# Ten small moves around a TensorE that hardly waits: gate total, identity transposes, unit 2, one eviction, one h and one rank sum

## The chip, the cores and the metric

The kernel runs on one core of a Trainium2 chip. The metric is the device time of one execution in microseconds (us), the median of several runs. Four engines do the work: TensorE (PE, matmuls; its weight loads are shown as PEld), VectorE (DVE), ScalarE (ACT) and GpSimd (POOL). SyncE (SP) issues most of the transfers (DMA) from the chip's memory. The engines run side by side and wait for each other through semaphores. TensorE's clock has two levels, 1.2 and 2.4 GHz; the profile shows the granted clock as a share of the higher one.

## The reference

`L0_attn_x` has 1024 tokens of 512 numbers. Three parts share the layernorm `xn`: a block whose weights come from 4-bit codes (NF4) with scales and low-rank additions, a feed-forward block whose weights are a mean plus one coefficient times a sign, and a product of the two.

```python
xn = layernorm(x)                                   # 1024 x 512
# block 1: dequantised weights W = NF4[codes] * scales, each with a low-rank term A, B
q, k, v = lin_lora(xn, Wq), lin_lora(xn, Wk), lin_lora(xn, Wv)
x1 = xn + lin_lora((q + k + v) / 3, Wo)
s  = x1 + lin_lora(silu(lin_lora(x1, Wg)) * lin_lora(x1, Wu), Wd)   # inner width 1792
# block 2: each of the three weights is one of these
def binary_diff_weight(w, base):
    d = w - base
    coeff = mean(abs(d))                            # one number for the whole weight
    return base + coeff * sign(d)
h = silu(xn @ W1.T) * (xn @ W3.T)                   # inner width 1792
g = silu(h @ W2.T)
out = x + s * g
```

## The kernel before, in words

The activations lie transposed, 512 features in four blocks of 128 rows (hc 0 to 3) and 1024 tokens in two halves of 512 (th 0 and 1). Every value that TensorE reads is split into a high and a low part, so that a full-precision product is three matmuls (high by high, high by low, low by high). A matmul group of one chunk of 128 inner rows and one half is 4 x 3 = 12 matmuls of 128 x 512.

The inner width of 1792 is 14 chunks for the feed-forward block (chunks 0 to 13) and 14 for the NF4 block (chunks 14 to 27, `B0` = 14). The order is written out by hand, engine by engine; there is no scheduler. Each engine has one list of instructions, and an instruction that waits holds up all behind it on its engine.

**The head.** VectorE computes the layernorm's statistics and normalises eight token tiles (`normalise(t)`), TensorE transposes them against an identity matrix (`ident`), ScalarE copies the high part out (`x_high`), VectorE subtracts to get the low part (`x_low`, counted by the semaphore `xT_lo`). Between these, TensorE runs `warm(bank, count)`: transposes of the identity whose result nobody reads. While the weights still come in, the three coefficients are summed: the first four chunks of each weight are "units" (unit 0 to 3 gate, 4 to 7 up, 8 to 11 down), the rest is scanned (`scan_subtract`, `scan_signs`, sums of absolute values on ScalarE or VectorE). GpSimd subtracts some units (`unit_subtract`), and `early_low` makes the low part of the mean of chunk 0; it waits for `scan_subtract(1)`.

The coefficient of the gate weight is not known when TensorE could begin. So chunk 0's gate is computed in two: `early_mean(th)` multiplies by the mean, 12 matmuls each, and `early_signs(th)` by the signs, 8 matmuls each, 16 in all; then `total(GATE)`, one small matmul with a matrix of ones, sums the partial sums over the rows. VectorE turns its result into the coefficient (`take_coeff`), makes unit 1 (`split_make`, `split_low`) and joins the two products of chunk 0 (`early_scale`, `early_add`), for ScalarE's `silu(0, th)`. The same with `total(UP)`, which stands in the middle of the gate matmuls of chunk 4, and `total(DOWN)`. The sums that `total` reads are ready when `take_part` has run on VectorE; it waits for all sums of that weight, the last on ScalarE is `unit_sum(7)` for the up weight.

`unit_make(u)` adds coefficient times sign (VectorE), `unit_high(u)` copies the high part (ScalarE), `unit_low(u)` makes the low part (VectorE); then `project(u, ...)` may start on TensorE.

**The middle and the end.** `STAGES` lists the order: a number is a phase (gate and up products of a chunk), "D0" to "D9" are down products of a group of two or three chunks, "X" makes x1. In a phase of the NF4 block VectorE has, beside `h_make` and `h_low` (the product of the two branches and its low part, for th 0 and 1), four "bends" (`nf4_bend`, 1536 wide, each on a ramp that ScalarE made) and one scaling (`nf4_scale`) that dequantise a later chunk, `rank_part` (`rank_add` and `lora_add`: the low-rank product that TensorE has just put into two banks is added), and `gu_low` and `dn_low`, the low parts of the next chunk's weights. `rank_gu` on TensorE may write its banks when ScalarE has evicted the down tiles that lay there (`y_evict`).

The lines that the steps below touch: the head's list on VectorE and on ScalarE (each written as plain calls), the start of TensorE's list with `WARM`, and in `phase(k)` on VectorE

```python
                if BEFORE[k] == k - 1:
                    h_make(k - 1, 1)
                    third_scale(k - 1)
                make(k)
                steps(k, 0)
                if BEFORE[k] == k - 1:
                    h_low(k - 1, 1)
                ...
                rank_part(k)
                ...
                steps(k, 1, 0, 1)
                split(k)
```

Of the kernel before, what the change touches and what calls it, by code (L numbers as in the profile page):

```python
# [10 lines left out]
TT = TOKENS // P  # L11
# [25 lines left out]
RING = 5  # L37
WARM = {-1: 12, 1: 8, 3: 5, 7: 7}
FIRST_TILES = 3
# [33 lines left out]
DOWN_RING = [(DOWN2, DOWN0, DOWN1, GATE0, GATE1) if g == 0 else (DOWN0, DOWN1, DOWN2, UP0, UP1) if g == FFN_GROUPS - 1  # L73
             else (DOWN0, DOWN2, UP0, DOWN1, UP1) for g in range(len(GROUPS))]
LATE_PHASES = [B0 + 1, B0 + 2, B0 + 3, B0 + 4]

# [69 lines left out]
def block_kernel(nc, x, xT_in, w_in, mean_in, codes_in, scales_in, codes_attn, scale_qkv_in, scale_o_in,  # L146
# [9 lines left out]
    with ctx:  # L156
# [530 lines left out]
        def _(act):  # L687
# [215 lines left out]
            def down_stage(g):  # L903
# [3 lines left out]
                steps(stage, 0)  # L907
                for t in range(TT):
                    y_evict(g, t)
                    if g == 0:  # L910
# [8 lines left out]
                    elif t >= 4 and stage == "D3":  # L919
                        steps(stage, 1, t, t + 1 if t < TT - 1 else None)  # L920
                    elif t == 1:
                        if stage in SPLIT_IN:
                            gu_high(SPLIT_IN[stage])
                    elif t == 2:
                        steps(stage, 1, 1, 2)
                    elif t == 3:
                        if stage in SPLIT_IN:
                            dn_high(SPLIT_IN[stage])
                    else:
                        steps(stage, 1, t - 2, t - 1 if t < TT - 1 else None)  # L930
# [56 lines left out]
            split_high(1)  # L987
            scan_signs(3)
            unit_signs(3)
            silu(0, 0)  # L990
            unit_high(2)
            silu(0, 1)
            scan_signs(4)
            silu(1, 0)
# [83 lines left out]
        def _(dve):  # L1078
# [298 lines left out]
            def phase(k):  # L1377
                if BEFORE[k] == k - 1:
                    h_make(k - 1, 1)
                    third_scale(k - 1)  # L1380
                make(k)
                steps(k, 0)
                if BEFORE[k] == k - 1:
                    h_low(k - 1, 1)
                if k == FIRST + 1:
                    dn_low(k)
                rank_part(k)
                if k == FIRST:
# [11 lines left out]
                if k - 1 in LATE_PHASES:  # L1400
                    late_low_rows(LATE_PHASES.index(k - 1))
                    h_low(k, 0)
                for s in ATTN_STEPS[k][1][2:3]:
                    attn_step(s)
                for s in NF4_STEPS[k][1][2:3]:
                    nf4_bend(s)
                if k - 1 not in LATE_PHASES:
# [85 lines left out]
            for t in range(4, TT):  # L1493
                normalise(t)
            scan_subtract(1)
            for t in range(4):
                x_low(t)
# [14 lines left out]
            split_low(1)  # L1512
            early_scale(0)
            early_add(0)
            early_scale(1)
            unit_make(2)
            early_add(1)
            scan_subtract(5)
            unit_low(2)
            unit_make(3)  # L1520
# [101 lines left out]
        def _(pe):  # L1622
# [3 lines left out]

            pe.wait_ge(const_ready, 3)
            warm(side_ps, WARM[-1])
            for t in range(TT):
# [5 lines left out]
                if t in (1, 3):  # L1635
                    warm(side_ps, WARM[t])
            pe.wait_ge(xT_lo, 1)
            warm(early_ps[0], WARM[TT - 1])

# [10 lines left out]
            def early_signs(th):  # L1650
                pe.wait_ge(unit_sign, 1)
                for hc in range(HC):
                    for x_part in (HI, LO):
                        last = nc.tensor.matmul(up_ps[th][:, :], sign_T[:, hc * P:(hc + 1) * P],
# [206 lines left out]
            early_signs(0)  # L1861
            total(GATE)
            early_signs(1)
# [84 lines left out]
```

## Time and profile before

| | |
|---|---|
| median of 3 runs | 536.0 us (535.98 to 536.23) |
| the profiled execution | 536.4 us, span 534.6 us |
| PE busy | 522.1 us, 98% of the span, 2337 matmuls |
| DVE busy | 442.0 us, 83% |
| ACT busy | 328.5 us, 61% |
| POOL busy | 94.8 us, 18% |
| mean granted clock of PE | 0.997 |

The span is the time from the first to the last instruction in the trace, and the execution's own time is 1.8 us longer. A busy share says little where engines take turns: what counts is when TensorE stands still, or runs at the lower clock, and who ended that wait.

### The profile page before, as it was taken

The numbers are of one execution on the slowest core, as the hardware profiler recorded it, in microseconds if no ns is written. First come the engines' busy times: TensorE is split into PE (matmuls) and PEld (weight loads), VectorE is DVE, ScalarE is ACT, GpSimd is POOL, SyncE is SP. The second block draws the span as 40 slices with busy tenths as digits, with TensorE's granted clock in tenths as the row PEclk, the third lists the DMA queues.
The fourth block names the chain that finished last, engine by engine and source line by source line (L and its number), as shares of the span: only waits on it lengthen the run. The fifth ranks groups of instructions, "written<-read, shape, count | busy, mean of one in ns | idle before, by whom it ended". The sixth has DMA issues, their size and how long they took to land.

```text
span 534.6 us, 6499 instructions
## 1 busy us (share of the span) xinstructions
PE 522.1 (98%) x2337; PEld 432.2 (81%) x2337; DVE 442.0 (83%) x520; ACT 328.5 (61%) x455; POOL 94.8 (18%) x106
## 2 busy tenths in 40 slices
PE   5899999999999999999999999999999999999997
PEld 4678888888888888888888888887888888888886
DVE  6988998988896998865898988999989898874446
ACT  2979978557546555446648557867876585464310
POOL 1311002003100310022003121300310040004590
PEclk9899999999999999999999999999999999999999
DMA  8999904045811491059238994932582377127503
GB/s 337 397 402 403 377 4 154 25 132 99 189 50 63 70 229 58 1 104 224 51 75 159 243 219 100 195 83 63 97 163 58 75 157 148 29 51 161 135 20 139
DMA packets 31744, 76.73 MB, mean 144 GB/s; under 512 B 3872, under 2 KB 7296, under 8 KB 31584
## 3 DMA queue, kind: packets, MB, share of 16 engines
q1 hardware_dynamic: 21632, 57.42, 34.4%
q0 software_dynamic: 9792, 18.88, 20.4%
q8 instruction: 19, 0.31, 0.2%
q14 instruction: 13, 0.11, 0.1%
q10 hardware_dynamic: 288, 0.02, 0.0%
HBM read 53.23 MB, written 2.10 MB: 103 GB/s over the span
## 4 chain that ended last, share of the span: by engine, by line
PE 87%; DVE 8%; issue 3%; DMA 1%; ACT 1%; SPq 0%; DVEq 0%; ACTq 0%
PE up_ps L1692 25%; PE gate_pair L1692 22%; PE down_pair L1733 10%; PE up_ps L1733 9%; PE down_ps L1733 7%; PE side_ps L1776 2%; PE down_pair L1692 2%; DVE acc L1339 2%; PE down_pair L1645 1%; PE up_ps L1853 1%; PE gate_pair L1853 1%; PE down_pair L1853 1%; DMA xn<-in_x 1%; PE down_pair L1815 1%; PE gate_pair L1733 1%
## 5 line engine op out<-in xcount | busy, mean ns | idle before, releaser
L1692 PE MATMUL up_ps<-xT,gu 128*128 128x512 f32 x648 | 152.3, 390 | 0.4 <-DVE gu L1173 0.2
L1692 PE MATMUL gate_pair<-xT,gu 128*128 128x512 f32 x624 | 148.4, 390 | 0.0
L1692 PEld LDWEIGHTS up_ps<-xT,gu 128*128 128x128 f32 x648 | 121.4, 188 | 26.4 <-DVE gu L1173 0.6
L1692 PEld LDWEIGHTS gate_pair<-xT,gu 128*128 128x128 f32 x624 | 117.0, 188 | 24.6 <-DVE gu L1164 0.5
L651 POOL DMA_DIRECT2D y<-y_part x64 | 55.3, 875 | 339.9 <-ACT y_part L815 338.7
L802 ACT ACTIVATE h<-up_ps 128x512 fp32r<-128x512 f32 x52 | 31.0, 597 | 111.1 <-DVE up_ps L1231 58.0
L861 ACT ACTIVATE ramp<-codes,bend_bias 128x1536 f32<-128x1536 uint8 x56 | 88.1, 1579 | 0.9 <-DMA codes<-in_codes 0.9
L1339 DVE SCALAR_TENSOR_TENSOR acc<-ramp,acc 128x1536 f32<-128x1536 f32 x42 | 73.7, 1754 | 4.4 <-ACT ramp L861 4.0
L1733 PE MATMUL down_pair<-h,dn 128*128 128x512 f32 x249 | 60.9, 389 | 0.0
L1733 PEld LDWEIGHTS down_pair<-h,dn 128*128 128x128 f32 x249 | 46.7, 188 | 9.8
L1236 DVE TENSOR_TENSOR h<-up_ps,h 128x512 fp32r<-128x512 f32 x52 | 35.8, 689 | 19.7 <-ACT h L802 19.4
L1733 PE MATMUL up_ps<-h,dn 128*128 128x512 f32 x210 | 51.5, 389 | 0.0
L1733 PEld LDWEIGHTS up_ps<-h,dn 128*128 128x128 f32 x210 | 39.4, 188 | 8.2
L1733 PE MATMUL down_ps<-h,dn 128*128 128x512 f32 x159 | 39.2, 390 | 0.0
L841 ACT ACTIVATE attn_ramp<-attn_codes,bend_bias 128x1024 f32<-128x1024 uint8 x32 | 36.8, 1150 | 0.0
L797 ACT ACTIVATE silu_gate<-gate_pair 128x512 f32<-128x512 f32 x48 | 28.3, 589 | 12.9 <-PE gate_pair L1692 12.7
L1733 PEld LDWEIGHTS down_ps<-h,dn 128*128 128x128 f32 x159 | 29.9, 188 | 6.1
L1292 DVE SCALAR_TENSOR_TENSOR attn_acc<-attn_ramp,attn_acc 128x1024 f32<-128x1024 f32 x24 | 29.3, 1220 | 3.0 <-ACT attn_ramp L841 2.9
L1339 DVE SCALAR_TENSOR_TENSOR acc<-ramp,codes 128x1536 f32<-128x1536 f32 x14 | 24.5, 1753 | 4.4 <-ACT ramp L861 4.4
L1231 DVE SCALAR_TENSOR_TENSOR up_ps<-up_ps,silu_gate 128x512 f32<-128x512 f32 x28 | 19.4, 693 | 9.2 <-PE up_ps L1692 9.2
L1349 DVE SCALAR_TENSOR_TENSOR acc<-acc,scale 128x1536 f32<-128x1536 f32 x14 | 24.6, 1756 | 0.4
L815 ACT ACTIVATE y_part<-up_ps 128x512 f32<-128x512 f32 x23 | 13.9, 603 | 12.5 <-PE up_ps L1733 12.5
(227 smaller groups left out, 648.1 us busy)
## 6 DMA issues: line engine op xcount, KB each, us to landing
y<-y_part POOLq DMA_DIRECT2D x64, 256.0 KB, 5.0
scale<-in_scales SPq DMA_DIRECT2D x28, 384.0 KB, 5.5
scan_w<-in_w SPq DMA_DIRECT2D x15, 512.0 KB, 10.9
base<-in_mean SPq DMA_DIRECT2D x9, 768.0 KB, 4.8
scan_mean<-in_mean SPq DMA_DIRECT2D x9, 512.0 KB, 9.7
silu_gate<-in_mean SPq DMA_DIRECT2D x6, 512.0 KB, 12.2
codes<-in_codes SPq DMA_DIRECT2D x14, 192.0 KB, 5.6
xn<-in_x SPq DMA_DIRECT2D x4, 512.0 KB, 4.9
```

What stands on the lines that cost most here:

```text
L651: pool.dma_start((y if g < FFN_GROUPS else y2)[:, hq, sl], y_slot(q), accum_op=ALU.add).then_inc(y_added[q % Y_SLOTS], 16)
L797: nc.scalar.activation(silu_buf(k, th), ps[:, :], ACT.Silu, scale=1.0 if k < B0 else UNIT_STEP).then_inc(silu_done, 1)
L802: nc.scalar.activation(h_part(k, HI, th), up_bank(k, th)[:, :], ACT.Copy).then_inc(h_hi, 1)
L841: nc.scalar.activation(attn_ramp[:, s % 2, :, :], attn_codes[:, a % 2, :, :], ACT.Prelu, bias=bend_bias[:, j:j + 1], scale=slope, alpha=le ...
L861: nc.scalar.activation(ramp[:, s % 2, :], codes[:, k % 2, :], ACT.Prelu, bias=bend_bias[:, j:j + 1], scale=slope, alpha=left).then_inc(nf4 ...
L1231: nc.vector.scalar_tensor_tensor(up_ps[th][:, :], up_ps[th][:, :], UNIT_STEP, silu_buf(k, th), ALU.mult, ALU.mult).then_inc(h_made, 1)
L1236: nc.vector.tensor_tensor(h_part(k, LO, th), up_bank(k, th)[:, :], h_part(k, HI, th).bitcast(f32), ALU.subtract).then_inc(h_lo, 1)
L1292: nc.vector.scalar_tensor_tensor(attn_acc[:, a % 2, :, :], attn_ramp[:, s % 2, :, :], end, attn_codes[:, a % 2, :, :] if j == 0 else attn_ ...
L1339: nc.vector.scalar_tensor_tensor(acc[k % 3][:, :], ramp[:, s % 2, :], end, codes[:, k % 2, :] if j == 0 else acc[k % 3][:, :], ALU.min if ...
L1349: nc.vector.scalar_tensor_tensor(acc[k % 3][:, :], acc[k % 3][:, :], UNIT_START, scale[:, :], ALU.add, ALU.mult).then_inc(nf4_scaled, 1)
L1692: last = nc.tensor.matmul(ps[:, :], w[:, w_part, hc * P:(hc + 1) * P], xT[:, x_part, hc, th * HALF:(th + 1) * HALF], start=(hc == 0 and w_ ...
L1733: last = nc.tensor.matmul(down_bank(g, t)[:, :], dn[:, k % DN_SLOTS, w_part, hq * P:(hq + 1) * P], h_part(k, h_p, th), start=(k == ks[0] a ...
```

## The change

In the head: the identity transposes go from 12 ahead of the first tile, 8 after the second, 5 after the fourth and 7 after the eighth to 8, 8, 7 and 18. The first 8 wait for the first half of the statistics (`ln_step`), and the last 18 come as 12, 3 and 3 after the first, second and third `x_low`. `x_low(0)` comes ahead of `scan_subtract(1)` on VectorE. `total(GATE)` moves from behind the first sign product into the second one, behind its fourth matmul. `unit_make(2)` and `unit_low(2)` come ahead of both `early_add`, and `scan_subtract(5)` comes between these two; on ScalarE `unit_high(2)` comes ahead of `silu(0, 0)`, and `scan_signs(4)` ahead of `silu(0, 1)`.

Later: in "D4" the eviction of tile 6 comes ahead of the ramp of the stage's fourth NF4 step. For phase 18, `rank_part` comes one phase earlier (in phase 17, ahead of the bend that stood there, which moves into phase 18), and `h_make(18, 1)` and `h_low(18, 1)` come ahead of a bend and of a scaling.

```diff
-WARM = {-1: 12, 1: 8, 3: 5, 7: 7}
+WARM = {-1: 8, 1: 8, 3: 7}
+WARM_LOW = {1: 12, 2: 3, 3: 3}
...
+H_AHEAD = [18]
+RANK_AHEAD = [18]
...
                 for t in range(TT):
+                    if stage == "D4" and t == 6:
+                        y_evict(g, t)
+                        steps(stage, 1, 3, 4)
+                        continue
                     y_evict(g, t)
...
-                    else:
+                    elif stage != "D4" or t != 5:
                         steps(stage, 1, t - 2, t - 1 if t < TT - 1 else None)
...
             scan_signs(3)
+            unit_high(2)
             unit_signs(3)
             silu(0, 0)
-            unit_high(2)
+            scan_signs(4)
             silu(0, 1)
-            scan_signs(4)
             silu(1, 0)
...
             def phase(k):
-                if BEFORE[k] == k - 1:
+                if k - 1 in H_AHEAD:
+                    h_low(k - 1, 1)
+                    third_scale(k - 1)
+                elif BEFORE[k] == k - 1:
                     h_make(k - 1, 1)
-                    third_scale(k - 1)
+                    if k not in RANK_AHEAD:
+                        third_scale(k - 1)
                 make(k)
                 steps(k, 0)
-                if BEFORE[k] == k - 1:
+                if BEFORE[k] == k - 1 and k - 1 not in H_AHEAD:
                     h_low(k - 1, 1)
...
-                rank_part(k)
+                if k in RANK_AHEAD:
+                    for s in NF4_STEPS[k - 1][1][2:3]:
+                        nf4_bend(s)
+                        nf4_scale(s)
+                else:
+                    rank_part(k)
...
+                if k in H_AHEAD:
+                    h_make(k, 1)
                 for s in ATTN_STEPS[k][1][2:3]:
                     attn_step(s)
-                for s in NF4_STEPS[k][1][2:3]:
-                    nf4_bend(s)
+                if k + 1 in RANK_AHEAD:
+                    rank_part(k + 1)
+                else:
+                    for s in NF4_STEPS[k][1][2:3]:
+                        nf4_bend(s)
...
                 normalise(t)
+            x_low(0)
             scan_subtract(1)
-            for t in range(4):
+            for t in range(1, 4):
                 x_low(t)
...
             early_scale(0)
+            unit_make(2)
+            early_scale(1)
+            unit_low(2)
             early_add(0)
-            early_scale(1)
-            unit_make(2)
+            scan_subtract(5)
             early_add(1)
-            scan_subtract(5)
-            unit_low(2)
             unit_make(3)
...
             pe.wait_ge(const_ready, 3)
+            pe.wait_ge(ln_step, 1)
             warm(side_ps, WARM[-1])
...
-            pe.wait_ge(xT_lo, 1)
-            warm(early_ps[0], WARM[TT - 1])
+            for low, count in WARM_LOW.items():
+                pe.wait_ge(xT_lo, low)
+                warm(early_ps[0], count)
...
             def early_signs(th):
                 pe.wait_ge(unit_sign, 1)
                 for hc in range(HC):
+                    if th == 1 and hc == 2:
+                        total(GATE)
...
             early_signs(0)
-            total(GATE)
             early_signs(1)
```

TensorE's list at the end of the head, before: the last identity transposes (`L1625`), the mean product (`L1645`, both halves), the sign products (`L1654`) with the total (`L1661`) between them, and the gate of chunk 1 (`L1692`).

```order
L1625 MATMUL down_pair<-ident 128x128 x7
L1645 MATMUL down_pair<-xT,gu 128x512 x24
L1654 MATMUL up_ps<-xT,dn 128x512 x8
L1661 MATMUL side_ps<-abs_part,ones 128x1
L1654 MATMUL up_ps<-xT,dn 128x512 x8
L1692 MATMUL gate_pair<-xT,gu 128x512 x24
```

The same place in the changed kernel; the names are the same, the line numbers have moved on.

```order
L1647 MATMUL down_pair<-ident 128x128 x18
L1669 MATMUL down_pair<-xT,gu 128x512 x24
L1680 MATMUL up_ps<-xT,dn 128x512 x12
L1687 MATMUL side_ps<-abs_part,ones 128x1
L1680 MATMUL up_ps<-xT,dn 128x512 x4
L1718 MATMUL gate_pair<-xT,gu 128x512 x24
```

The total now has twelve sign matmuls ahead of it and four behind it, where it had eight and eight.

VectorE's list behind the coefficient, before: `early_scale` (`TENSOR_SCALAR`), `early_add` (`down_pair`), `unit_make(2)` (the first `unit_st`), `scan_subtract(5)`, `unit_low(2)` (`gu`), `unit_make(3)`.

```order
L1476 TENSOR_SCALAR silu_gate<-up_ps,coeff 128x512
L1481 TENSOR_TENSOR down_pair<-down_pair,silu_gate 128x512
L1476 TENSOR_SCALAR silu_gate<-up_ps,coeff 128x512
L1148 SCALAR_TENSOR_TENSOR unit_st<-unit_st,coeff 128x512
L1481 TENSOR_TENSOR down_pair<-down_pair,silu_gate 128x512
L1084 TENSOR_TENSOR scan_w<-scan_w,scan_mean 128x1024
L1173 TENSOR_TENSOR gu<-unit_st,gu 128x512
L1148 SCALAR_TENSOR_TENSOR unit_st<-unit_st,coeff 128x512
```

The same instructions in the changed kernel.

```order
L1497 TENSOR_SCALAR silu_gate<-up_ps,coeff 128x512
L1155 SCALAR_TENSOR_TENSOR unit_st<-unit_st,coeff 128x512
L1497 TENSOR_SCALAR silu_gate<-up_ps,coeff 128x512
L1180 TENSOR_TENSOR gu<-unit_st,gu 128x512
L1502 TENSOR_TENSOR down_pair<-down_pair,silu_gate 128x512
L1091 TENSOR_TENSOR scan_w<-scan_w,scan_mean 128x1024
L1502 TENSOR_TENSOR down_pair<-down_pair,silu_gate 128x512
L1155 SCALAR_TENSOR_TENSOR unit_st<-unit_st,coeff 128x512
```

The low part of unit 2 has moved from seventh to fourth, and the second `early_add` from fifth to seventh, behind the scan.

VectorE's list at the passage from phase 17 to phase 18, before: `h_low(17, 0)`, the first bend of a chunk (`acc<-ramp,codes`), `h_make(17, 1)`, `h_low(17, 1)`, `rank_add`, `lora_add`, the next bend, `gu_low(19)`.

```order
L1236 TENSOR_TENSOR h<-up_ps,h 128x512
L1339 SCALAR_TENSOR_TENSOR acc<-ramp,codes 128x1536
L1231 SCALAR_TENSOR_TENSOR up_ps<-up_ps,silu_gate 128x512
L1236 TENSOR_TENSOR h<-up_ps,h 128x512
L1215 TENSOR_TENSOR acc<-acc,down_pair 128x4x2x128
L1221 TENSOR_TENSOR acc<-acc,side_ps 128x512
L1339 SCALAR_TENSOR_TENSOR acc<-ramp,acc 128x1536
L1202 TENSOR_TENSOR gu<-acc,gu 128x2x512
```

The same place in the changed kernel.

```order
L1243 TENSOR_TENSOR h<-up_ps,h 128x512
L1222 TENSOR_TENSOR acc<-acc,down_pair 128x4x2x128
L1228 TENSOR_TENSOR acc<-acc,side_ps 128x512
L1238 SCALAR_TENSOR_TENSOR up_ps<-up_ps,silu_gate 128x512
L1243 TENSOR_TENSOR h<-up_ps,h 128x512
L1346 SCALAR_TENSOR_TENSOR acc<-ramp,codes 128x1536
L1346 SCALAR_TENSOR_TENSOR acc<-ramp,acc 128x1536
L1209 TENSOR_TENSOR gu<-acc,gu 128x2x512
```

The rank sum has moved ahead of the second half of h, and the two bends of the same accumulator now follow each other directly.

## Rows read from the trace of the kernel before

**Rows 1.** The page, busy time of each engine.

```profile
PE 522.1 (98%) x2337; PEld 432.2 (81%) x2337; DVE 442.0 (83%) x520; ACT 328.5 (61%) x455; POOL 94.8 (18%) x106
```

**Rows 2.** PE timeline of the head: start, length, engine, line, [idle before <-releaser].

```profile
18.87 0.98 PE L1625 MATMUL down_pair<-ident 128*128 128x128 f32 x7 [1.08 <-DVE xT L1129]
20.75 7.34 PE L1645 MATMUL down_pair<-xT,gu 128*128 128x512 f32 x24 [0.90 <-DVE xT L1129]
...
29.75 0.28 PE L1661 MATMUL side_ps<-abs_part,ones 128*128 128x1 f32 x2
...
32.01 5.73 PE L1692 MATMUL gate_pair<-xT,gu 128*128 128x512 f32 x24
37.95 5.74 PE L1692 MATMUL up_ps<-xT,gu 128*128 128x512 f32 x24 [0.21 <-DVE gu L1173]
43.52 5.60 PE L1692 MATMUL down_pair<-xT,gu 128*128 128x512 f32 x24
...
51.01 0.28 PE L1661 MATMUL side_ps<-abs_part,ones 128*128 128x1 f32 x2
```

**Rows 3.** Stretches: length, busy PE, PEld, DVE, ACT, POOL, clock, DMA, GB/s.

```profile
14.30:17.80 3.50, 2.91 (x24) 2.32 (x22) 3.50 (x6) 3.48 (x6) 0.00 (x0) 1.00 1.03 411
17.80:21.00 3.20, 1.23 (x8) 1.02 (x9) 3.20 (x6) 3.20 (x7) 2.63 (x3) 1.00 1.03 412
21.10:24.40 3.30, 3.30 (x9) 2.58 (x8) 3.30 (x6) 3.02 (x8) 2.14 (x2) 0.50 1.03 402
...
37.10:49.40 12.30, 12.09 (x53) 9.69 (x52) 12.21 (x14) 12.14 (x25) 2.60 (x2) 1.00 1.03 404
```

**Rows 4.** DVE timeline of the head.

```profile
16.99 1.22 DVE L1084 TENSOR_TENSOR scan_w<-scan_w,scan_mean 128x1024 f32<-128x1024 f32 x1
...
21.72 1.49 DVE L1084 TENSOR_TENSOR scan_w<-scan_w,scan_mean 128x1024 f32<-128x1024 f32 x1
...
23.73 0.68 DVE L1129 TENSOR_TENSOR xT<-side_ps,xT 128x512 fp32r<-128x512 f32 x1
...
32.26 0.74 DVE L1476 TENSOR_SCALAR silu_gate<-up_ps,coeff 128x512 f32<-128x512 f32 x1
...
35.57 1.72 DVE L1084 TENSOR_TENSOR scan_w<-scan_w,scan_mean 128x1024 f32<-128x1024 f32 x1
...
49.46 0.16 DVE L1136 TENSOR_REDUCE abs_part<-abs_sums 128x1 f32<-128x9 f32 x1
```

**Rows 5.** POOL timeline of the head.

```profile
19.61 2.52 POOL L637 TENSOR_TENSOR unit_st<-unit_st 128x512 f32<-128x512 f32 x2
...
34.42 1.79 POOL L637 TENSOR_TENSOR unit_st<-unit_st 128x512 f32<-128x512 f32 x1 [9.84 <-DMA unit_st<-in_mean]
```

**Rows 6.** ACT timeline of the head, `silu(1, 0)`.

```profile
37.13 0.59 ACT L797 ACTIVATE silu_gate<-gate_pair 128x512 f32<-128x512 f32 x1
```

**Rows 7.** Timeline of all engines at the end of stage D4.

```profile
293.14 1.60 ACT L861 ACTIVATE ramp<-codes,bend_bias 128x1536 f32<-128x1536 uint8 x1
...
294.62 0.60 ACT L815 ACTIVATE y_part<-down_pair 128x512 f32<-128x512 f32 x1
...
295.27 0.53 PEld L1815 LDWEIGHTS down_pair<-B_gu,A_gu 96*128 96x128 f32 x4 [0.47 <-ACT y_part L815]
```

**Rows 8.** DVE timeline of phases 17 and 18 and stage D6.

```profile
352.97 1.75 DVE L1339 SCALAR_TENSOR_TENSOR acc<-ramp,codes 128x1536 f32<-128x1536 f32 x1
...
359.99 1.22 DVE L1202 TENSOR_TENSOR gu<-acc,gu 128x1024 fp32r<-128x1024 f32 x1
...
387.75 3.62 DVE L1339 SCALAR_TENSOR_TENSOR acc<-ramp,acc 128x1536 f32<-128x1536 f32 x2
```

**Rows 9.** PE timeline of phase 19.

```profile
361.61 5.60 PE L1692 MATMUL gate_pair<-xT,gu 128*128 128x512 f32 x24
367.05 2.88 PE L1692 MATMUL up_ps<-xT,gu 128*128 128x512 f32 x12
370.12 3.01 PE L1692 MATMUL up_ps<-xT,gu 128*128 128x512 f32 x12 [0.19 <-DVE h L1236]
```

## The prediction

> **What bounds the kernel now.** I read the page first: PE is busy for 98% of the span [rows 1], so only its waits and its stretches at the lower clock can be won, and whatever holds it up elsewhere costs the full amount. The table of waits names few ends of PE's idle time, so I went to its timeline in the head [rows 2] and to the two later places that the change touches [rows 7 to 9].
>
> The reader is to see four things in [rows 2] and [rows 3]. First, the mean product takes 7.34 us for 24 matmuls where a later group of 24 takes 5.60: from 21.1 to 24.4 the granted clock is 0.50. The stretch ahead of it had PE busy for 1.23 of 3.20 us. Second, the gate total runs at 29.75 and the gate of chunk 1 starts at 32.01, 2.26 us later: total, coefficient, make, high and low part follow each other on VectorE and ScalarE with nothing to shorten them. Third, the gate of chunk 2 waits at 37.95 for the low part of unit 2. Fourth, the up total at 51.01 comes 1.4 us after its sums were ready (49.46 plus 0.16 [rows 4]).
>
> A group's normal spacing is 5.44 us (361.61 to 367.05 [rows 9]), 0.227 a matmul. After a stall a group is longer: 37.95 to 43.52 is 5.57, so a restart costs 0.13 on top of the wait.
>
> **The head, up to the gate total.** Adding identity transposes costs little: 7 took 0.98, 0.14 each with the last one's tail. The 18 fit into the gaps in which PE waits for `x_low`: PE has done its last tile at about 17.8, and the mean product starts at 20.75 only because the fourth `x_low` ends just ahead. `x_low(0)` is moved ahead of `scan_subtract(1)`, but the sum of work up to the fourth `x_low` is the same, so 20.75 stays. If the cover were gone (clock low while they run), they would take twice as long and delay the mean by up to 1 us.
>
> With them PE is busy for some 2.3 of those 3.2 us. The stretch 14.3 to 17.8, with 2.91 of 3.50 busy and transposes alone, was followed by full clock; 1.23 of 3.20 was followed by half. I take it that the clock stays up, as 2.3 of 3.2 (0.72) lies nearer to 0.83 than to 0.38.
>
> The Trainium skill (TensorE: Matmul & The Clock Gate, Part 4: PE-mode transpose) says that work in transpose mode does not count as busy in the same way and does not bring the full clock. The trace speaks against it, since the 24 PE instructions of 14.3 to 17.8 are all transposes and the clock was 1.00. By the page the time would be that of the last rival below.
>
> What does the full clock give? The first half of the mean product ends at 20.75 + 0.1 + 12 x 0.227 = 23.6. The second half reads the second half of the tokens, whose last `x_low` ended at 23.73 + 0.68 = 24.41 [rows 4]; at the lower clock PE came later than that, so nobody saw this wait. Now it is the next wait: PE starts at 24.5. From there to the total the old order has 20 matmuls (12 mean, 8 sign), the new one 24: 24 x 0.227 + 0.1 = 5.55, so the total runs at 30.05, 0.3 **later** than before, though the clock is doubled. In the old place it would run at 29.1. The four matmuls cost 0.9, since everything behind the total hangs on it.
>
> There is a second delay. GpSimd's `early_low` waits for `scan_subtract(1)`, which now comes one `x_low` later, 0.60 us. GpSimd then runs three subtractions without a gap, two of them in the row of 2.52 us from 19.61 [rows 5], the last one until 22.13. `scan_subtract(2)` at 21.72 took 1.49 instead of 1.22 (16.99 [rows 4]): it lay for 0.41 us under GpSimd's. The one at 35.57 lay under GpSimd's for 0.64 (34.42 + 1.79 = 36.21) and took 1.72, 0.50 more. So the extra is the overlap less 0.14. With GpSimd 0.60 later the overlap is 1.01, the extra 0.87, against 0.27 before: the last `x_low` ends 0.60 later still, and the total runs at 30.65, **0.9 later**. If the overlap does not grow, it is 0.3; those are the bounds. I take 0.9, since two rows show the same relation. And if the clock does fall at 21.1 as before, the second half of the mean isn't late, and the four matmuls alone cost 0.9: the same value by another way.
>
> **Unit 2 and the up total.** Moving `unit_low(2)` ahead takes it from 37.2 to about 5 us behind the total, 2 us ahead of its need. The stall at 37.95 is gone: 32.01 to 37.95 is 5.94, a restarted group is 5.57, so 0.37 plus the restart of 0.13, **0.5 won** there.
>
> But `early_add(1)` and with it `silu(0, 1)` are late. Counted from the total's start: `early_scale(0)` at 2.5 (32.26), `unit_make(2)` 0.7 later, then ScalarE's `unit_high(2)` between make and low (0.74 + 0.63 and two hand-overs), so `unit_low(2)` at 4.6; half a microsecond under GpSimd's subtraction, which `scan_subtract(5)` paid before; `early_add(0)` at 5.7, `scan_subtract(5)` at 6.3, `early_add(1)` at 7.4 to 8.1; then `silu(0, 1)` and at 8.6 `silu(1, 0)`. Before, `silu(1, 0)` was at 37.13 [rows 6], 7.4 behind the total. ScalarE is 1.2 us late from there, and between 37.1 and 49.4 it is busy for 12.14 of 12.30 us, VectorE for 12.21 [rows 3]: nothing takes that up, and VectorE waits for ScalarE's `unit_high(3)`, so it is as late. The up sums are ready at 49.62 + 1.2 = 50.85 (counted on the old total), and PE, 0.5 ahead, is there at 50.5 and waits until 50.9. Of the 0.5 only **0.1** is left; the bounds are 0 and 0.5. The waiting total holds up PE's whole queue.
>
> The head's sum is 0.9 - 0.1 = +0.8.
>
> **D4 and phases 17 to 19.** The eviction of tile 6 at 294.62 holds up the rank matmuls (0.47 at the weight loads, some 0.3 in PE's spacing). It moves ahead of the ramp at 293.14 [rows 7]: 0.3 won. The ramp is 0.48 later (an eviction's turn), and VectorE's bend waits for each ramp, so VectorE is 0.48 later from 295 on; up to phase 18 it and ScalarE wait only for each other, so it stays late.
>
> In phase 17 the rank sum changes places with a bend. From 352.97 to the low part of chunk 19 at 359.99 [rows 8] VectorE has the same instructions in either order, but the two bends of one accumulator now follow directly: two such take 3.62, 1.87 from start to start instead of 1.67, so 0.2 more. `gu_low(19)` ends at 359.99 + 1.22 + 0.48 + 0.2 = 361.9. PE needs it at 361.61 [rows 9], or at 361.3 with the 0.3 won: a new stall of 0.6 and 0.13. In return `h_low(18, 1)` is a bend and a scaling earlier, and the stall at 370.12 goes (367.05 + 12 x 0.227 = 369.77, so 0.35 and 0.13). Sum: -0.3 + 0.7 - 0.5 = **-0.1**, bounds -0.8 (VectorE not late) and +0.4. Behind it VectorE is 0.7 late, with waits of 2 us to take it up.
>
> **The sum.** 0.8 - 0.1 = +0.7 on the profiled execution's 536.4 (span 534.6 and 1.8 around it): 537.1. The median of the runs is 536.0, 0.4 below that execution, so I forecast **536.7**. About 0.2%, 1.07 us, is what a measurement of this kernel can tell from no change; the forecast lies within it.
>
> **The rivals.**
> - The waits behind do not come (GpSimd does not delay `scan_subtract(2)`, or ScalarE catches up): for it speaks that the rows show each only once or twice. +0.3 or +0.9 - 0.5, less 0.1: 536.1 to 536.3. Chance 0.2.
> - All stalls taken out stay out: 0.3 - 0.5 - 0.8 = -1.0, 535.0. It needs VectorE at its old times at 49.5 and at 361. Chance 0.07.
> - Slower: the clock falls in the new gap ahead of the mean's second half (23.6 to 24.5 or 25.1). The one fall cost 7.34 - 5.60 = 1.7. [...] 536.7 + 1.7 = 538.4. Chance 0.12.
> - The transposes do nothing for the clock. Then 18 of them take 0.21 to 0.28 each, the mean starts up to 1 us later and at the lower clock: 536.7 + 1.0 = 537.7. This is what the page's rule would do; chance 0.05.
>
> **How the numbers follow.** The forecast with its own spread (536.3 to 537.2) has 0.5; the rest, 0.06, is for waits that I did not see. Over 537.07 lie the two slow rivals, the forecast's upper edge and some of the rest: 0.25. Under 534.93 lies half of the second rival at most and a little of the rest: 0.05. Same: 0.7. The range from 535.7 to 537.8 leaves out the clock's fall and the case of 535.0.
>
> **What would show it.** Right: granted clock 1.00 from 20.8 on; the mean product split by a wait near 24.5 to 25.1; the gate total near 30.6; no wait at 38; a wait at the up total near 51.8; a wait ahead of chunk 19's gate, none in its up product. Wrong: a gate total before 29.7, an up total that doesn't wait, or a clock of 0.50 in 24.5 to 28.

## The result, and the profile after

| | before | changed |
|---|---|---|
| median of 11 runs | 536.09 us (535.93 to 536.59) | 537.38 us (537.29 to 537.54) |
| the profiled execution | 536.4 us, span 534.6 | 537.38 us, span 535.5 |
| mean granted clock in it | 0.997 | 1.000 |

The changed kernel takes 1.0023 times as long (95% interval 1.0014 to 1.0032): slower by 1.3 us. The forecast of 536.7 us was 0.7 short. The time lies within the stated range of 535.7 to 537.8, but the rise of 1.29 is more than the 1.07 us that the prediction took as the least that can be told from no change.

The page, busy time of each engine (before: [rows 1]):

```profile
PE 519.4 (97%) x2346; PEld 430.2 (80%) x2346; DVE 443.5 (83%) x520; ACT 328.8 (61%) x455; POOL 94.4 (18%) x106
```

PE is busy for 2.7 us less, and the span is 0.9 us longer: the work went faster (the mean product alone takes 5.97 instead of 7.34), and the waits grew by more.

The stretches of the head (before: [rows 3]). The columns are the length, the busy time of PE, PEld, DVE, ACT and POOL, the granted clock, the DMA share and GB/s.

```profile
17.80:21.00 3.20, 2.80 (x20) 2.12 (x20) 3.20 (x5) 3.20 (x7) 2.01 (x2) 1.00 1.03 414
21.10:24.40 3.30, 2.64 (x12) 1.86 (x10) 3.30 (x5) 2.40 (x6) 2.14 (x3) 1.00 1.04 403
37.10:49.40 12.30, 12.30 (x56) 10.20 (x55) 11.06 (x12) 11.97 (x21) 2.59 (x2) 1.00 1.03 403
```

The granted clock stays at 1.00. In the third stretch PE no longer waits, and now VectorE does (11.06 busy where it was 12.21).

PE's timeline of the head, changed kernel (start, length, engine, line, operation, and in brackets the idle time before it and who ended it; before: [rows 2]):

```profile
17.75 1.53 PE L1647 MATMUL down_pair<-ident 128*128 128x128 f32 x12
19.49 1.14 PE L1647 MATMUL down_pair<-ident 128*128 128x128 f32 x6 [0.20 <-DVE xT L1136]
20.77 2.97 PE L1669 MATMUL down_pair<-xT,gu 128*128 128x512 f32 x12
25.19 3.00 PE L1669 MATMUL down_pair<-xT,gu 128*128 128x512 f32 x12 [1.44 <-DVE xT L1136]
28.03 2.88 PE L1680 MATMUL up_ps<-xT,dn 128*128 128x512 f32 x12
30.75 0.28 PE L1687 MATMUL side_ps<-abs_part,ones 128*128 128x1 f32 x2
30.89 1.18 PE L1680 MATMUL up_ps<-xT,dn 128*128 128x512 f32 x4
33.03 5.76 PE L1718 MATMUL gate_pair<-xT,gu 128*128 128x512 f32 x24 [0.96 <-DVE gu L1171]
38.62 5.60 PE L1718 MATMUL up_ps<-xT,gu 128*128 128x512 f32 x24
44.06 5.60 PE L1718 MATMUL down_pair<-xT,gu 128*128 128x512 f32 x24
49.50 2.20 PE L1718 MATMUL gate_pair<-xT,gu 128*128 128x512 f32 x9
51.81 0.38 PE L1687 MATMUL side_ps<-abs_part,ones 128*128 128x1 f32 x2
52.05 3.65 PE L1718 MATMUL gate_pair<-xT,gu 128*128 128x512 f32 x15
```

The mean product runs at full speed and then waits 1.44 us for the last `x_low`. The gate total comes at 30.75 instead of 29.75, the gate of chunk 1 at 33.03 instead of 32.01. The wait at chunk 2 is gone (38.62, with no bracket), and the up total at 51.81 is only 0.80 later than before. It does wait: nine matmuls from 49.50, at 0.227 each, are through at 51.54, and its sums are ready at 51.75 (51.59 and 0.16 in the next rows), so PE stands for 0.27.

VectorE's rows that answer to [rows 4], and `unit_low(3)`, which now waits:

```profile
21.74 2.11 DVE L1091 TENSOR_TENSOR scan_w<-scan_w,scan_mean 128x1024 f32<-128x1024 f32 x1
...
24.37 0.68 DVE L1136 TENSOR_TENSOR xT<-side_ps,xT 128x512 fp32r<-128x512 f32 x1
...
35.39 1.00 DVE L1180 TENSOR_TENSOR gu<-unit_st,gu 128x512 fp32r<-128x512 f32 x1
...
42.39 0.69 DVE L1180 TENSOR_TENSOR gu<-unit_st,gu 128x512 fp32r<-128x512 f32 x1 [1.21 <-ACT gu L753]
...
51.59 0.16 DVE L1143 TENSOR_REDUCE abs_part<-abs_sums 128x1 f32<-128x9 f32 x1
```

GpSimd's subtractions (before: [rows 5]) and ScalarE's `silu(1, 0)` (before: [rows 6]):

```profile
20.22 2.55 POOL L640 TENSOR_TENSOR unit_st<-unit_st 128x512 f32<-128x512 f32 x2
...
34.52 1.33 POOL L640 TENSOR_TENSOR unit_st<-unit_st 128x512 f32<-128x512 f32 x1 [9.31 <-DMA unit_st<-in_mean]
```

```profile
39.26 0.59 ACT L800 ACTIVATE silu_gate<-gate_pair 128x512 f32<-128x512 f32 x1
```

`scan_subtract(2)` lies under GpSimd's two subtractions until 22.77 and takes 2.11 us. ScalarE comes to `silu(1, 0)` 2.1 us later than before, 1.1 of it beyond the delay of the total.

VectorE and PE at the passage from phase 17 to phase 19 (before: [rows 8, 9]):

```profile
358.05 1.75 DVE L1346 SCALAR_TENSOR_TENSOR acc<-ramp,codes 128x1536 f32<-128x1536 f32 x1
359.91 1.76 DVE L1346 SCALAR_TENSOR_TENSOR acc<-ramp,acc 128x1536 f32<-128x1536 f32 x1
361.59 1.22 DVE L1209 TENSOR_TENSOR gu<-acc,gu 128x1024 fp32r<-128x1024 f32 x1
```

```profile
356.75 5.60 PE L1718 MATMUL up_ps<-xT,gu 128*128 128x512 f32 x24
...
362.86 5.76 PE L1718 MATMUL gate_pair<-xT,gu 128*128 128x512 f32 x24 [0.51 <-DVE gu L1209]
368.45 5.60 PE L1718 MATMUL up_ps<-xT,gu 128*128 128x512 f32 x24
```

There is a new wait ahead of chunk 19's gate, and the 24 matmuls of its up product run through, where before they were split at 370.12.

### The profile page after: what moved, and what is told of

It reads as the page before. It is cut to its first block, busy times and chain, and to the rows that moved or that the text cites. A ratio compares the mean times of both kernels' runs of the same rounds, so it can differ in the third digit from the quotient of the medians.

```text
span 535.5 us, 6518 instructions
## 1 busy us (share of the span) xinstructions
PE 519.4 (97%) x2346; PEld 430.2 (80%) x2346; DVE 443.5 (83%) x520; ACT 328.8 (61%) x455; POOL 94.4 (18%) x106
## 4 chain that ended last, share of the span: by engine, by line
PE 89%; DVE 7%; issue 2%; ACT 1%; DMA 1%; SPq 0%; DVEq 0%
PE up_ps L1718 25%; PE gate_pair L1718 25%; PE down_pair L1759 11%; PE up_ps L1759 9%; PE down_ps L1759 7%; PE side_ps L1802 2%; DVE scan_w L1091 1%; PE up_ps L1879 1%; PE gate_pair L1879 1%; PE down_pair L1879 1%; PE down_pair L1718 1%; DMA xn<-in_x 1%; PE down_pair L1841 1%; PE gate_pair L1759 1%; PE down_pair L1774 1%
```

## The experiments

Each was timed beside the kernel before, whose median was 536.1 to 536.2 each time. None leaves out work that the result needs. "Changed" is the changed kernel's 537.38.

**1. The gate total back in its place**, all else as changed.

```diff
-                    if th == 1 and hc == 2:
-                        total(GATE)
...
             early_signs(0)
+            total(GATE)
             early_signs(1)
```

> The changed kernel with the gate total back behind the first sign product (eight sign matmuls ahead of it instead of twelve), all else as changed. Theory: the four sign matmuls ahead of the total cost 0.9 us and all that follows up to the up total hangs on it: gate total at 29.85 instead of 30.75, gate of chunk 1 at 32.1 instead of 33.03, up total 0.9 earlier, time 537.4 - 0.9 = 536.5. Rival: the later part of the head is set by transfers or by ScalarE's own list, so that the up total stays at 51.8: 537.4.

Measured: 536.68, 0.70 less. The gate total is at 29.99 and the gate of chunk 1 at 32.26, in a trace whose first statistics of the tokens on VectorE (their start waits for a transfer) stand at 4.52 instead of 4.33; so the total is 0.9 earlier, as expected. The up total still waits a little:

```profile
51.22 0.38 PE L1685 MATMUL side_ps<-abs_part,ones 128*128 128x1 f32 x2 [0.31 <-DVE abs_part L1143]
```

The four sign matmuls cost 0.9 at the total. 0.7 of it reaches the end; the rest stays in VectorE's list, where `scan_subtract(5)` now starts at 35.82, inside GpSimd's subtraction, and takes 1.72.

**2. The denser transposes alone**, on the kernel before, with the change's waits for `ln_step` and `xT_lo` ahead of them.

```diff
-WARM = {-1: 12, 1: 8, 3: 5, 7: 7}
+WARM = {-1: 8, 1: 8, 3: 7}
+WARM_LOW = {1: 12, 2: 3, 3: 3}
```

> The kernel before with the denser identity transposes alone (8, 8, 7 and 12 + 3 + 3); x_low(0), the total, unit 2 and the later edits stay as before. Theory: the granted clock stays at 1.00 and the gate total comes at 29.2 instead of 29.75, but GpSimd's unit subtraction at 34.4 does not move, so scan_subtract(5) lies under it for 1.2 us instead of 0.64 and takes 2.2 to 2.3 instead of 1.72; the low part of unit 2 and PE's restart at 38 come no earlier: 536.0 to 536.1, no change. Rival 1: all that follows the total moves with it: 536.1 - 0.55 = 535.5. Rival 2: without the moved x_low(0) the transposes leave a wider gap and the clock falls as before: total at 29.75, 536.1.

Measured: 536.12, ratio 0.9998 (0.9990 to 1.0007). The number is that of the theory, the reason is not. VectorE and GpSimd:

```profile
35.33 1.72 DVE L1085 TENSOR_TENSOR scan_w<-scan_w,scan_mean 128x1024 f32<-128x1024 f32 x1
```

```profile
34.42 1.55 POOL L638 TENSOR_TENSOR unit_st<-unit_st 128x512 f32<-128x512 f32 x1 [9.52 <-DMA unit_st<-in_mean]
```

The scan does not grow: GpSimd's subtraction had itself been held up by `unit_make(2)`, which now ends earlier, so it ends at 35.97 instead of 36.21. Measured from the first statistics on VectorE (4.60 here, 4.28 before) PE is some 0.6 earlier from the gate total to the end of the trace. Then why is the time the same? The runs of the kernel before answer it. Of its 33 runs beside this experiment 14 had a mean granted clock of 1.000 and a median of 536.04, 12 had 0.997 and 536.38, and 7 had 0.993 or 0.994 and 536.08. The profile that I had read is one of the 0.997 (536.4). All 11 runs with denser transposes have 1.000, and none of the 120 runs of all kernels with them is under 0.999. I read this so: the fall of the clock in the mean product does not come in every run of the kernel before, but in about a third of them, and costs them 0.3; the median holds little or nothing of it. Two things stay open: only one run with 0.997 was profiled, so where the clock fell in the others is not shown, and the two traces differ by 0.6 where the medians by clock differ by 0.3.

**3. `x_low(0)` back behind `scan_subtract(1)`**, all else as changed.

```diff
-            x_low(0)
             scan_subtract(1)
-            for t in range(1, 4):
+            for t in range(4):
```

> The changed kernel with x_low(0) back behind scan_subtract(1) on VectorE. Theory: GpSimd's subtractions start 0.6 earlier, scan_subtract(2) takes 1.49 instead of 2.11, the mean's second half starts at 24.55 instead of 25.19 and the gate total comes at 30.1 instead of 30.75; all behind follows: 537.4 - 0.65 = 536.75. Rival: the clock falls at 21.1, since the first identity transposes behind the first x_low come later: the mean's first half takes 5.1, and the total comes at 30.75 or later: 537.4.

Measured: 537.32, 0.06 less. `scan_subtract(2)` takes 1.53, the mean's second half starts at 24.50, the total at 30.06, all as expected, and by the up total nearly all of it is lost. VectorE, GpSimd and PE:

```profile
34.68 1.58 DVE L1180 TENSOR_TENSOR gu<-unit_st,gu 128x512 fp32r<-128x512 f32 x1
```

```profile
34.42 1.30 POOL L640 TENSOR_TENSOR unit_st<-unit_st 128x512 f32<-128x512 f32 x1 [9.91 <-DMA unit_st<-in_mean]
```

```profile
51.68 0.38 PE L1686 MATMUL side_ps<-abs_part,ones 128*128 128x1 f32 x2 [0.69 <-DVE abs_part L1143]
```

GpSimd's subtraction of the next unit starts when its transfer lands, at 34.4 to 34.7 in every profile, whatever the total does. `unit_low(2)`, 0.7 earlier, starts inside it, takes 1.58 instead of 1.00, and with `early_add(0)` at 36.19 instead of 36.31 VectorE is where it was. PE, ahead by 0.7, waits for the sums. The theory was right as far as the total and wrong behind it. How narrow this is shows beside experiment 1, whose gate of chunk 1 starts at nearly the same time (32.26, here 32.32). Its `unit_low(2)` starts at 34.61, 0.07 ahead of GpSimd's subtraction (34.68 in that trace), and takes 0.69; its up total is at 51.22 instead of 51.68. Three of the 11 runs of experiment 1 take 537.07 to 537.24, the others 536.46 to 536.68; whether GpSimd came first in those three is not shown.

**4. Without the D4 edit**, all else as changed.

```diff
-                    if stage == "D4" and t == 6:
-                        y_evict(g, t)
-                        steps(stage, 1, 3, 4)
-                        continue
...
-                    elif stage != "D4" or t != 5:
+                    else:
```

> The changed kernel without the edit in D4 (the eviction of tile 6 behind the fourth step's ramp, as before). Theory: PE waits 0.3 more at 296 for the rank matmuls, but VectorE is 0.48 earlier from there on, the low part of chunk 19's weights comes in time and PE's stall of 0.78 at 362.9 goes: 537.4 + 0.33 - 0.78 = 536.9 to 537.0. Rival: the ramp's delay does not reach phase 19 (the stall there is the rank sum's alone): 537.4 + 0.33 = 537.7.

Measured: 537.35, no change; neither theory nor rival. VectorE is 0.49 earlier from D4 on, but in phase 17 it waits for PE's rank product ahead of `rank_add`, and PE's stall at chunk 19 comes to its end at the same moment as in the changed kernel:

```profile
354.35 1.22 DVE L1218 TENSOR_TENSOR acc<-acc,down_pair 128x1024 f32<-128x1024 f32 x1 [0.40 <-PE down_pair L1837]
```

```profile
362.86 1.43 PE L1714 MATMUL gate_pair<-xT,gu 128*128 128x512 f32 x5 [0.20 <-DVE gu L1205]
```

**5 and 6. Of the later edits only the earlier h of phase 18 (5), and all but the earlier rank sum (6).**

```diff
-RANK_AHEAD = [18]
+RANK_AHEAD = []
```

Experiment 5 takes back the D4 edit as well, as in experiment 4.

> The changed kernel without the D4 edit and without the earlier rank sum of phase 18, so that of the later edits only the earlier h of phase 18 is left. Theory: the eviction's delay on VectorE and the rank sum's wait for PE each hold the low part of chunk 19's weights late by themselves, and only without both does PE's stall of 0.78 at 362.9 go, while 0.33 comes back at 296: 537.4 + 0.33 - 0.78 = 536.9 to 537.0. Rival: the stall at chunk 19 comes from the h edit: it stays with one or both of the others undone, 537.4 to 537.7.

> The changed kernel with the rank sum of phase 18 back in phase 18; the D4 edit and the earlier h stay. Theory: the two bends of one accumulator no longer follow each other (0.2), but VectorE is still 0.49 late from D4 on, so PE's stall ahead of chunk 19's gate shrinks from 0.67 to some 0.45: 537.4 - 0.2 = 537.2. Rival: the stall is the rank sum's alone and goes: 537.4 - 0.78 = 536.6.

Measured: 536.82 and 537.14, so 0.56 and 0.24 less, both by the theory. PE ahead of chunk 19's gate, first in 5, then in 6:

```profile
362.51 5.60 PE L1714 MATMUL gate_pair<-xT,gu 128*128 128x512 f32 x24
```

```profile
362.69 2.56 PE L1718 MATMUL gate_pair<-xT,gu 128*128 128x512 f32 x10 [0.32 <-DVE gu L1209]
```

With experiment 4: the eviction's delay and the rank sum's place each keep `gu_low(19)` late, and taking one back leaves the other.

**7. `scan_subtract(5)` behind both early sums, `scan_signs(4)` ahead of `silu(0, 0)`**, all else as changed.

```diff
             early_add(0)
-            scan_subtract(5)
             early_add(1)
+            scan_subtract(5)
...
+            scan_signs(4)
             silu(0, 0)
-            scan_signs(4)
             silu(0, 1)
```

> The changed kernel with scan_subtract(5) behind the second early_add on VectorE, and scan_signs(4) ahead of silu(0, 0) on ScalarE (into its idle 1.2 us at 35.9). Theory: ScalarE is no longer 1.2 us late from silu(1, 0) on, unit_high(3) comes a microsecond earlier, VectorE's idle 1.2 us at 42.4 goes, the up sums are ready ahead of PE, and the wait of 0.26 and the restart of 0.1 at the up total go: 537.4 - 0.35 = 537.0. Rival: the up sums wait for transfers or for VectorE's own list: the up total stays at 51.8, 537.4.

Measured: 536.92, 0.46 less. The up total is at 51.49 and no longer split from the gate matmuls ahead of it; `unit_low(3)` starts at 41.39 instead of 42.39, after 0.23 of waiting for ScalarE instead of 1.21. So it was ScalarE's lateness, which the place of `scan_subtract(5)` and of `scan_signs(4)` brought, that held the up sums; the two places were not tried one by one.

**8. Unit 2, early sums and scan in the old order**, all else as changed; the edit is the difference that the change's order rows show, with ScalarE's list likewise.

> The changed kernel with unit 2, the early sums and scan_subtract(5) in the order of before on VectorE and ScalarE. Theory: with the gate total 1.0 late, scan_subtract(5) lies behind GpSimd's subtraction and takes 1.2 instead of 1.7, so the low part of unit 2 ends at 38.3, about when PE comes for it (38.6): no stall there, and ScalarE isn't 1.2 late, so the up total doesn't wait either: 537.4 - 0.35 = 537.0. Rival, by the prediction's sum: a stall of 0.5 at chunk 2 comes back and 0.4 at the up total goes: 537.5.

Measured: 537.24, 0.14 less, between the two. PE comes to chunk 2 at 38.66 after a small stall (its gate began at 32.94, and 5.57 behind that is 38.51) and to the up total at 51.71 without a wait. Moving unit 2 as the change does it brought nothing: the runs without it (537.04 to 537.50) overlap those of the changed kernel (537.29 to 537.54). The total's delay had already taken `scan_subtract(5)` out from under GpSimd (it takes 1.21).

**9 and 10. Three edits together**: unit 2 as in experiment 7, the earlier h of phase 18, and the denser transposes (9) or the old ones (10); total, `x_low(0)`, D4 and rank sum as before. VectorE's part of unit 2, against the kernel before:

```diff
             early_scale(0)
-            early_add(0)
-            early_scale(1)
             unit_make(2)
+            early_scale(1)
+            unit_low(2)
+            early_add(0)
             early_add(1)
             scan_subtract(5)
-            unit_low(2)
```

> The kernel before with three of the edits: the denser identity transposes, unit 2 ahead of the early sums (with scan_subtract(5) behind both and scan_signs(4) ahead of silu(0, 0)), and the earlier h of phase 18; total, x_low(0), D4 and the rank sum stay as before. Theory: gate total at 29.2 to 29.5, PE's stall of 0.36 and 0.11 at chunk 2 goes without a wait at the up total, and that of 0.38 and 0.11 in chunk 19's up product goes; nothing comes in their place: 536.1 - 0.47 - 0.47 = 535.2. Rival: the up sums become the bound with a total this early (GpSimd's subtraction at 34.4 lies over the low part of unit 2): the first 0.47 is given back at the up total, 535.6.

> The same three edits without the denser transposes: 12, 8, 5 and 7 as before. Theory: in most runs the clock does not fall while the mean product runs and the transposes are worth nothing there, so the median is that of the kernel with them, 535.1 to 535.2; about a third of the runs have a mean clock of 0.997 and are 0.3 longer. Rival, as the profile of before was read: the fall belongs to the sparse transposes and comes in every run, 535.2 + 0.3 to 0.5 = 535.5 to 535.7.

Measured: 534.91 (ratio 0.9975, 0.9966 to 0.9985) and 535.15 (0.9979, 0.9970 to 0.9988): faster than both kernels. PE's timeline of 9, from its longest run (535.33), which is the one profiled:

```profile
31.97 5.74 PE L1711 MATMUL gate_pair<-xT,gu 128*128 128x512 f32 x24
37.54 5.60 PE L1711 MATMUL up_ps<-xT,gu 128*128 128x512 f32 x24
...
50.47 0.28 PE L1680 MATMUL side_ps<-abs_part,ones 128*128 128x1 f32 x2
```

Neither chunk 2 nor the up total waits. This run is not the usual one: its gate total waits 0.23 for the sums and stands at 29.61, that of experiment 10 at 29.15. The stretches of 10:

```profile
8.40:15.10 6.70, 5.95 (x27) 5.55 (x28) 6.49 (x18) 3.74 (x7) 0.61 (x1) 0.50 1.01 389
...
17.80:21.00 3.20, 1.30 (x9) 1.05 (x10) 3.20 (x6) 3.20 (x7) 2.70 (x3) 1.00 1.03 413
21.10:24.40 3.30, 2.59 (x12) 1.77 (x10) 3.30 (x6) 3.12 (x8) 2.14 (x2) 1.00 1.04 407
```

PE is busy for 1.30 of 3.20 us, as little as in [rows 3], and the next stretch still has the clock at 1.00. Of its 11 runs, three with a mean clock of 0.996 or 0.997 take 535.39 to 535.66 and the others 534.87 to 535.29. So the denser transposes are worth some 0.4 in about a quarter of the runs, and little in the median.

**11. The changed kernel with few transposes.**

```diff
-WARM_LOW = {1: 12, 2: 3, 3: 3}
+WARM_LOW = {1: 7}
```

> The changed kernel with 7 identity transposes instead of 18 ahead of the mean product, all else as changed. Theory: the runs spread over several mean clocks as those of the kernel before do; in the undisturbed ones nothing changes (537.4); where the clock falls during the mean's first half, this takes up to 5.2 instead of 2.75 us and ends 0.6 behind the low part for which the second half waits, so those runs take up to 538.0. Median 537.4. Rival: with x_low(0) early and the gap ahead of the mean's second half, the clock falls in every run: 538.0 or more.

Measured: 537.36. Three of 11 runs have a mean clock of 0.997 and take 537.32 in the median, no longer than the rest. The 0.6 that the theory gave to a fall did not show: where in the head it fell in those three runs was not seen, since the profiled run has 1.000.

**12. Experiment 9 with `x_low(0)` moved ahead**, as the change has it.

> The kernel of the three edits (unit 2 with scan_subtract(5) late, the earlier h, the denser transposes) with x_low(0) moved ahead of scan_subtract(1), as the change has it. Theory: the move delays GpSimd's subtractions by 0.6, scan_subtract(2) takes 2.1 instead of 1.5, and the gate total comes 0.65 later; undoing it in the changed kernel gained nothing only because the up sums waited behind GpSimd's subtraction there. Here the up sums have a microsecond to spare, so the whole 0.65 shows: 534.9 + 0.65 = 535.55. Rival: the move costs nothing anywhere (0.06 in the changed kernel): 534.9 to 535.0.

Measured: 535.57, 0.66 more than experiment 9, by the theory. The gate total is at 29.74, 0.59 later than in experiment 10, the better one to compare with, since the profiled run of 9 was its longest. VectorE and PE:

```profile
21.66 2.10 DVE L1087 TENSOR_TENSOR scan_w<-scan_w,scan_mean 128x1024 f32<-128x1024 f32 x1
```

```profile
25.11 2.98 PE L1665 MATMUL down_pair<-xT,gu 128*128 128x512 f32 x12 [1.43 <-DVE xT L1132]
```

So the move of `x_low(0)` costs 0.66 where the up sums have time to spare, and its removal gains 0.06 where they don't (experiment 3).

## Why the prediction was right and where it was wrong

**The head, up to the gate total: right.** The prediction put the total at 30.65 and 0.9 late, by two steps: 0.3 from the four matmuls behind a late `x_low`, 0.6 from GpSimd lying longer over `scan_subtract(2)`. The trace has 30.75, 1.00 late, and 2.11 us for the scan, where the prediction's 1.22 and 0.87 make 2.09. Experiment 1 takes the first cause away by itself, experiment 3 the second, and experiment 12 adds the second alone. The Trainium skill (SBUF — State Buffer, SBUF: two separate sides) calls the ports that VectorE and GpSimd share an exclusive lock: whoever starts first has them for the whole instruction. The rows agree: the three long ones (2.11, 1.58, 1.72) each started inside a GpSimd subtraction and took their usual time (1.22, 0.68, 1.22) and what was left of GpSimd's less 0.14, as the prediction had it; `early_add` at 34.73 in experiment 2, one of whose inputs lies in PSUM (the banks that TensorE writes), took its usual 0.69 there.

**Unit 2 and the up total: right.** 0.5 won at chunk 2 and 0.4 given back were forecast. The group behind chunk 2 starts at 44.06 instead of 43.52, so of the 1.02 at chunk 1's gate 0.54 are left there: 0.48 won. Behind the up total PE is at 52.05, where it was at 51.14 before:

```profile
51.14 3.67 PE L1692 MATMUL gate_pair<-xT,gu 128*128 128x512 f32 x15
```

That is 0.91 late, so 0.37 came back. Experiment 7 shows that the give-back was ScalarE's, as said. (The prediction's 49.62 + 1.2 is 50.82, not 50.85; nothing hangs on it.)

**D4 and phases 17 to 19: sizes right, one cause missed.** PE's up product of chunk 17 is 0.58 late (356.75 against 356.17), 0.33 less than behind the up total (0.91); the wait of 0.47 at the rank weights [rows 7] is gone. Chunk 19's gate costs 0.8 (forecast 0.7), and the stall in its up product gives back some 0.5 (forecast 0.5; the end of the up product is at 374.05 instead of 373.13 [rows 9]). The sum is 0.0 where -0.1 was forecast. But the new stall was put down to the eviction's 0.48 and the bends' 0.2 as a sum. Experiments 4 to 6 show that the rank sum's place holds VectorE back by itself, because it waits for PE's rank product until 354.35 (experiment 4): without the eviction nothing is gained, without the rank sum 0.24, without both 0.56.

**The step that failed** is the last: "The median of the runs is 536.0, 0.4 below that execution, so I forecast **536.7**." The prediction subtracted the 0.4 as if the changed kernel's median would lie as far below its own profiled execution. Most of it goes with the clock's fall, which the profiled execution of before had and its median run has not (536.38 at a mean clock of 0.997, 536.04 at 1.000). The change takes the fall away, so its own profiled execution is its median, 537.38. The 0.7 by which the forecast fell short are these 0.4, another 0.2 in the sum of the terms (0.9 against 0.8 in the head, 0.0 against -0.1 behind it), and 0.1 outside the span (1.9 instead of 1.8). That the time still came to lie in the range is owed to its width, not to this step.

**The clock.** That the transposes keep it up was right: all runs of experiment 2 are at 1.000. That the sparse ones let it fall, as "1.23 of 3.20 was followed by half" had it, does not hold in every run: 1.30 of 3.20 in experiment 10 was followed by 1.00. What decides it from run to run stays open. Neither of the two rivals that hung on the clock came: it was 1.00 through the gap ahead of the mean's second half and through the 18 transposes. The rule of the Trainium skill that the prediction weighed (TensorE: Matmul & The Clock Gate, Part 4: PE-mode transpose) finds no support in these runs: with transposes alone ahead of it, the mean product of experiment 2 ran its first 12 matmuls in 3.00 us at a granted clock of 1.00, and the mean clock was 1.000 in all 11 runs.

## What to carry to other kernels

Before an event of one profiled run is priced, look whether that run's time and mean clock are those of the median: a gain that takes away what only some runs have is no gain in the median, and its price must not be subtracted twice. Taking back one of several edits can show nothing because the next wait stands at the same moment; experiments 3 and 4 gained 0.06 and 0.03, though the same causes cost 0.66 (experiment 12 against 9) and 0.32 (6 against 5) in other company. And where an engine's work starts when a transfer lands, moving the other engines in time moves them in or out from under it: the GpSimd subtraction at 34.4 to 34.7, 1.3 to 1.8 us long, decided what the edits of the total, of `x_low(0)` and of unit 2 were worth.

## What was not expected of the hardware

- The moment at which PE's clock rises or falls in the head is not the kernel's alone: 33 runs of one program gave mean granted clocks of 1.000 (14), 0.997 (12) and 0.993 or 0.994 (7). A mean clock of 0.993 cost nothing (536.08 against 536.04), one of 0.997 cost 0.3. In the profiled run of experiment 10, with 0.994, the clock was at 0.50 from 8.4 to 15.1, and at 1.00 in the mean product.
- A listed clock of 1.00 near the start of a trace need not mean that PE ran at it. The kernel before, then experiment 10; the first line is a stretch of the kernel before, with the clock third from the end:

```profile
9.20:11.00 1.80, 1.78 (x9) 1.78 (x10) 1.80 (x4) 0.60 (x1) 0.61 (x1) 1.00 1.02 407
9.22 1.97 PE L1632 MATMUL down_pair<-ident,xn 128*128 128x128 f32 x8 [4.72 <-DVE xn L1124]
15.77 1.12 PE L1632 MATMUL gate_pair<-ident,xn 128*128 128x128 f32 x8 [0.58 <-DVE xn L1124]
```

```profile
9.15 1.97 PE L1649 MATMUL down_pair<-ident,xn 128*128 128x128 f32 x8 [4.64 <-DVE xn L1127]
15.70 1.11 PE L1649 MATMUL gate_pair<-ident,xn 128*128 128x128 f32 x8
```

  Eight transposes of a tile take 1.97 us at 9.2 in both, at a listed 1.00 in the one and 0.50 in the other, and 1.1 us at 15.7. So the kernel before ran them no faster than experiment 10 did at half the clock, and only the trace of experiment 10 lists it. This fits that a mean clock of 0.993 cost nothing. In every profile the transposes come to the shorter time somewhere between 10.4 and 15.2 us, while PE has run nothing but transposes.
- A VectorE instruction can hold GpSimd's up as well as the other way about: the same subtraction of 128x512 took 1.27 to 1.31 alone, and 1.33, 1.55 and 1.79 where `unit_make(2)` ran on for another 0.16, 0.39 and 0.63 when it started (changed kernel, experiment 2, kernel before). `scan_subtract(5)` in the kernel before and in experiment 2, and `unit_low(2)` in the changed kernel, which VectorE came to while it still ran, were held up in their turn (1.72, 1.72 and 1.00).
